# PV matmuls of two steps in one block, bf16 pieces of the row maxima on GpSimd, and another order in the gating stage

## The reference, cut to what matters

```python
q, k, v = split(x @ W_qkv + b_qkv)            # 16 heads of 16
q, k = rope(q), rope(k)
att = where(causal, q @ k.T / 4, -1e9)
y = softmax(att) @ v @ W_proj + b_proj
x1 = layernorm(x + y)
probs = softmax(x1 @ gate_w.T); expert = argmax(probs)     # top 1 of 8
rank = cumsum(one_hot(expert)) - 1; keep = rank < 640
ffn = probs[expert] * (relu(x1[kept] @ w1 + b1) @ w2 + b2) # 0 for dropped tokens
out = layernorm(x1 + ffn)
```

## Time and profile before

| | us |
|---|---|
| median of 3 runs (lowest, highest) | 1422.44 (1416.7, 1422.6) |
| the profiled execution | 1421.05 |
| its span, first to last instruction | 1419.3 |
| mean granted TensorE clock | 0.94 |
| TensorE busy | 1271.5 (90%) |
| VectorE busy | 1158.4 (82%) |
| ScalarE busy | 777.7 (55%) |
| GpSimd busy | 230.3 (16%) |

### The profile page before, as it was taken

How to read it: one execution, slowest core, us unless ns; L and a number is a source line. 1 busy time by engine, 2 the same in 40 slices (tenths; PEclk the granted TensorE clock), 3 DMA queues, 4 the chain that set the end, 5 groups by cost and what they waited for, 6 DMA issues and landing times. The chain is left out here.

```text
span 1419.3 us, 22655 instructions
## 1 busy us (share of the span) xinstructions
PE 1271.5 (90%) x7857; PEld 644.2 (45%) x7857; DVE 1158.4 (82%) x2780; ACT 777.7 (55%) x1098; POOL 230.3 (16%) x250
## 2 busy tenths in 40 slices
PE   8892997999999999999999999999578739999997
PEld 4550132333333333333333333332366539999997
DVE  6994997999999999899899999991276728888886
ACT  2441065666666666666666667668245435544442
POOL 1336000100100100101101100101234321111221
PEclk9995599999999999999999999999888859999999
DMA  6877496131131131121221210000545422343330
GB/s 206 255 240 167 62 155 146 31 90 32 31 91 31 33 88 32 48 74 31 61 60 32 75 46 10 23 2 16 165 142 181 154 92 93 101 142 117 96 105 21
DMA packets 120272, 126.91 MB, mean 89 GB/s; under 512 B 16604, under 2 KB 102751, under 8 KB 120160
## 3 DMA queue, kind: packets, MB, share of 16 engines
q1 hardware_dynamic: 116576, 117.01, 29.7%
q0 software_dynamic: 3584, 8.47, 1.7%
HBM read 83.02 MB, written 48.38 MB: 93 GB/s over the span
## 5 line engine op out<-in xcount | busy, mean ns | idle before, releaser
L625 ACT ACTIVATE probs<-scores 128x1024 f32<-128x1024 f32 (+3 forms) x640 | 539.0, 894 | 327.9 <-PE scores L518 327.0
L680 DVE TENSOR_REDUCE part_max<-ring 128x1 f32<-128x512 f32 x768 | 478.4, 684 | 24.0 <-PE ring L548 22.4
L548 PE MATMUL ring<-k_stack,q_stack 96*128 96x512 bf16 (+3 forms) x1280 | 407.1, 363 | 41.1 <-DMA k_stack<-pieces_d 26.2
L518 PE MATMUL scores<-q_stack,k_stack 99*128 99x512 bf16 (+3 forms) x1280 | 339.8, 350 | 9.9 <-DMA q_stack<-max_rows 7.6
L534 PE MATMUL out_p<-probs,v_s 128*32 128x512 f32 (+3 forms) x2560 | 300.2, 541 | 0.5 <-POOL probs L730 0.3
L548 PEld LDWEIGHTS ring<-k_stack,q_stack 96*128 96x128 bf16 x1280 | 114.9, 97 | 347.9 <-DVE part_max L680 148.7
L674 DVE CUSTOM_DVE_ANT_0 scratch<-ring,mask_s 128x384 f32<-128x384 f32 (+2 forms) x384 | 195.0, 551 | 18.0 <-issue 17.1
L730 POOL TENSOR_SCALAR_AFFINE_SELECT probs<-probs 128x512 f32<-128x512 f32 x128 | 81.6, 637 | 781.8 <-ACT probs L625 781.8
L518 PEld LDWEIGHTS scores<-q_stack,k_stack 99*128 99x128 bf16 x1280 | 113.0, 98 | 182.7 <-issue 64.3
L1394 PE MATMUL psY<-w_hi,h_hi 128*128 128x256 f32 x320 | 90.9, 284 | 0.0
L534 PEld LDWEIGHTS out_p<-probs,v_s 128*32 128x32 f32 x2560 | 50.6, 108 | 87.3 <-issue 56.2
(11 more groups left out here) (113 smaller groups left out, 1349.9 us busy)
## 6 DMA issues: line engine op xcount, KB each, us to landing
w_whole<-w SPq DMA_DIRECT2D x16, 1024.0 KB, 7.5
q_stack<-pieces_d SPq DMA_DIRECT2D x192, 64.0 KB, 3.0
k_stack<-pieces_d SPq DMA_DIRECT2D x192, 64.0 KB, 3.1
v_d<-vt SPq DMA_DIRECT2D x8, 1024.0 KB, 4.6
v_s<-v_d SPq DMA_DIRECT2D x8, 1024.0 KB, 6.0
o_d<-o_s SPq DMA_DIRECT2D x32, 256.0 KB, 2.2
p_o<-o_d SPq DMA_DIRECT2D x8, 1024.0 KB, 6.0
slots_d<-no_row SPq DMA_DIRECT2D x1, 5200.0 KB, 28.3
```

Source lines behind the costliest of these rows:

```text
L518: last = nc.tensor.matmul(scores[p][:, hh, off:CHUNK], k_stack[i][0:KROWS, kb // TPC, j, kb % TPC * P:(kb % TPC + 1) * P], q_stack[i][0:KR ...
L548: last = nc.tensor.matmul(slot[:, h * w:(h + 1) * w], q_stack[i][0:SROWS, qt // TPC, j + h, qt % TPC * P:(qt % TPC + 1) * P], k_stack[i][0 ...
L625: nc.scalar.activation(probs[n % NPROB][:, 2 * p:2 * p + 2, off:CHUNK], scores[p][:, :, off:CHUNK], ACT.Exp, scale=SCALE).then_inc(exp_don ...
L680: nc.vector.tensor_reduce(part_max[:, qt, j, t:t + 1], ring[m % 3][:, 0:w], axis=AX.X, op=ALU.max).then_inc(ring_read, 1)
```

## The change

1. *PV.* `step` no longer calls PV for the step two before in every step. In each odd step it calls `pv_pair`, which runs PV for two steps one behind the other; even steps have none. `copy_o` on ScalarE moves from behind a step's two exponentials to between the two of the next step.
2. *Pieces.* VectorE only negates the turned maxima into SBUF (`negate_maxima`) and gives the ring slot back. GpSimd makes the three pieces (`cut_maxima`), placed in its stream by `PLAN`, behind the mask of the same step. SP waits for GpSimd's last piece instead of for the ring.
3. *Gating stage.* On ScalarE `deviations` is split; the second root stands behind the next chunk's first `copy_yT`, and `copy_x1T` and the plain rows are arranged anew. On VectorE `norm_chunk` goes ahead of `place`, and the next chunk's first `normalise` ahead of `choose`. On TensorE the next chunk's first `turn_o` goes ahead of the logits.

TensorE's order in the first unit, from one PV block on, before: two rows with `out_p` are the PV blocks of single steps (four heads each); `ring` are ring items, `scores` the scores of a step.

The diff:

```diff
@@ -326,7 +326,8 @@
 LAG = 2
-assert NSTEP % NPROB == 0
+PAIR = 2
+assert NSTEP % NPROB == 0 and all(last % PAIR == PAIR - 1 for last in LAST)
@@ -399,6 +400,7 @@
         row_max = [sb(f"row_max{c}", [P, NMAXROW]) for c in range(NCH)]
+        max_neg = [sb(f"max_neg{c}", [NMAXROW, P]) for c in range(NCH)]
         max_rest = sb("max_rest", [NMAXROW, P])
@@ -425,7 +427,7 @@
         MAX_PRIMED = [1 + MAX_DMAS] + [1] * (NCH - 1)
-        N_CUT = NPIECE
+        N_CUT = NPIECE + 1
@@ -449,9 +451,9 @@
-            def load_max(c, i, read):
...
-                sp.wait_ge(ring_read, read)
+            def load_max(c, i, uses):
...
+                sp.wait_ge(max_cut[c], N_CUT * uses)
                 for pc in range(NPIECE):
@@ -464,16 +466,16 @@
                 for c in (2, 1):
-                    load_max(c, i, NRING * u + TURN_AT[c] + 1)
+                    load_max(c, i, u + 1)
                 store_o(u, b, g, 3)
...
                     load_chunk(two_ahead[0], two_ahead[1], i, 3)
-                load_max(0, i, NRING * (u + 1) + (1 if last else TURN_AT[0] + 1))
+                load_max(0, i, u + 2)
                 store_o(u, b, g, 2)
...
                 if not last:
-                    load_max(3, 1 - i, NRING * (u + 1) + TURN_AT[3] + 1)
+                    load_max(3, 1 - i, u + 2)
                 for c in (1, 0):
@@ -486,7 +488,7 @@
             load_v(0, 0, 0)
-            load_max(3, 0, TURN_AT[3] + 1)
+            load_max(3, 0, 1)
             for c in ORDER:
@@ -587,20 +589,25 @@
                 if behind:
-                    pv_step(*behind)
+                    pv_pair(*behind)
                 items(u, i, uses, third, stop, ahead)
...
+            def pv_pair(u, i, n):
...
+                for m in range(n - PAIR + 1, n + 1):
+                    pv_step(u, i, m)
...
                         pe.wait_ge(v_loaded[i], 16 * uses[0])
-                    step(u, i, uses, n, ahead, (u, i, n - LAG))
-                for n in range(NSTEP - LAG, NSTEP):
-                    if ahead:
-                        step(u + 1, 1 - i, uses[1:], n + LAG - NSTEP, ahead, (u, i, n))
-                    else:
-                        pv_step(u, i, n)
+                    step(u, i, uses, n, ahead, (u, i, n - LAG) if n % PAIR else None)
+                if ahead:
+                    for n in range(LAG):
+                        step(u + 1, 1 - i, uses[1:], n, ahead, (u, i, NSTEP + n - LAG) if n % PAIR else None)
+                else:
+                    pv_pair(u, i, NSTEP - 1)
@@ -618,6 +625,12 @@
                 for p in range(2):
+                    if p == 1:
+                        if n == LAG and u:
+                            copy_o(u - 1, 0)
+                        for c in ORDER:
+                            if n - LAG - 1 == LAST[c]:
+                                copy_o(u, c)
                     act.wait_ge(scores_ready[p], NSTEP * u + n + 1)
@@ -630,18 +643,9 @@
-            def unit(u, follows):
+            for u in range(UNITS):
                 for n in range(NSTEP):
                     exp_step(u, n)
-                    if n == LAG - 1 and follows:
-                        copy_o(u - 1, 0)
-                    for c in ORDER:
-                        if n - LAG == LAST[c]:
-                            copy_o(u, c)
...
-            unit(0, False)
-            for u in range(1, UNITS):
-                unit(u, True)
             copy_o(UNITS - 1, 0)
@@ -688,47 +692,61 @@
-            def cut_maxima(c, u, m):
-                turned = ring[m % 3][0:NMAXROW, 0:P]
-                first, second, third = (rows[:] for rows in max_rows[c])
+            def negate_maxima(c, u, m):
+                if u:
+                    dve.wait_ge(max_cut[c], N_CUT * u)
                 dve.wait_ge(ring_full, NRING * u + m + 1)
...
-                dve.wait_ge(max_loaded[c], 1 + MAX_DMAS * u)
-                nc.vector.tensor_scalar(first, turned, -1.0, None, ALU.mult).then_inc(max_cut[c], 1)
-                dve.wait_ge(max_cut[c], N_CUT * u + 1)
-                nc.vector.scalar_tensor_tensor(max_rest[:], turned, -1.0, first,
-                                               ALU.mult, ALU.subtract).then_inc(max_cut[c], 1)
-                dve.wait_ge(max_cut[c], N_CUT * u + 2)
-                nc.vector.tensor_copy(second, max_rest[:]).then_inc(max_cut[c], 1)
-                dve.wait_ge(max_cut[c], N_CUT * u + 3)
-                nc.vector.tensor_tensor(third, max_rest[:], second, ALU.subtract).then_inc(ring_read, 1)
+                nc.vector.tensor_scalar(max_neg[c][:], ring[m % 3][0:NMAXROW, 0:P], -1.0, None,
+                                        ALU.mult).then_inc(ring_read, 1)
...
                     if isinstance(item, int):
-                        cut_maxima(item, u, m)
+                        negate_maxima(item, u, m)
                     else:
...
                         fold(u, FOLD_AFTER[m], m)
-            cut_maxima(0, UNITS, 0)
+            negate_maxima(0, UNITS, 0)
...
                 nc.gpsimd.memset(k_stack[i][SROWS:KROWS], 1.0).then_inc(ones_set, 1)
+            pool.wait_ge(const_loaded, 16 * 2)
...
+            def cut_maxima(c, u, m):
+                first, second, third = (rows[:] for rows in max_rows[c])
+                pool.wait_ge(max_loaded[c], 1 + MAX_DMAS * u)
+                pool.wait_ge(ring_read, NRING * u + m + 1)
+                nc.gpsimd.tensor_copy(first, max_neg[c][:]).then_inc(max_cut[c], 1)
+                pool.wait_ge(max_cut[c], N_CUT * u + 1)
+                nc.gpsimd.tensor_tensor(max_rest[:], max_neg[c][:], first, ALU.subtract).then_inc(max_cut[c], 1)
+                pool.wait_ge(max_cut[c], N_CUT * u + 2)
+                nc.gpsimd.tensor_copy(second, max_rest[:]).then_inc(max_cut[c], 1)
+                pool.wait_ge(max_cut[c], N_CUT * u + 3)
+                nc.gpsimd.tensor_tensor(third, max_rest[:], second, ALU.subtract).then_inc(max_cut[c], 1)
...
+            def mask(u, n):
+                off = STEPS[n][2]
+                for p in range(2):
+                    pool.wait_ge(exp_done[p], NSTEP * u + n + 1)
+                block_ = probs[n % NPROB][:, :, off:off + P]
+                nc.gpsimd.affine_select(out=block_, in_=block_, compare_op=ALU.is_ge, fill=0.0, base=0,
+                                        pattern=[[0, HPU], [1, P]], channel_multiplier=-1).then_inc(masked, 1)
...
+            for m in range(LEAD):
+                if isinstance(ITEMS[m], int):
+                    cut_maxima(ITEMS[m], 0, m)
             for u in range(0, UNITS):
-                for d, n in enumerate(DIAG):
-                    off = STEPS[n][2]
-                    done = in_register(pool, NSTEP * u + n + 1)
-                    pool.wait_ge(const_loaded, 16 * 2)
-                    for p in range(2):
-                        pool.wait_ge(exp_done[p], done)
...
-                    block_ = probs[n % NPROB][:, :, off:off + P]
-                    nc.gpsimd.affine_select(out=block_, in_=block_, compare_op=ALU.is_ge, fill=0.0, base=0,
-                                            pattern=[[0, HPU], [1, P]], channel_multiplier=-1).then_inc(masked, 1)
+                for n, (first, stop) in enumerate(PLAN):
+                    if n in DIAG:
+                        mask(u, n)
+                    for m in range(first, stop):
+                        v, k = u + m // NRING, m % NRING
+                        if isinstance(ITEMS[k], int) and (v < UNITS or k == TURN_AT[0]):
+                            cut_maxima(ITEMS[k], v, k if v < UNITS else 0)
@@ -973,10 +991,11 @@
                 project(n, 2)
+                if h_next is not None:
+                    turn_o(n + 1, 1 - i, h_next, 0)
                 gate_logits(n - 1)
...
                 if h_next is not None:
-                    turn_o(n + 1, 1 - i, h_next, 0)
                     turn_o(n + 1, 1 - i, h_next, 1)
@@ -1007,9 +1026,11 @@
-            def deviations(n, i):
+            def first_root(n, i):
                 act.wait_ge(mv_ready, TPC * (n + 1))
                 nc.scalar.activation(std[i][:], mv[i][:, :, 1], ACT.Sqrt, bias=eps_s[:]).then_inc(std_ready, 1)
...
+            def second_root(n, i):
                 act.wait_ge(var_step, 2 * (n + 1))
@@ -1033,22 +1054,24 @@
                 copy_yT(n, 0)
+                second_root(n - 1, 1 - i)
+                copy_yT(n, 1)
                 plain_rows(n - 1, 1 - i, h_before, (0, 1))
-                copy_yT(n, 1)
+                copy_yT(n, 2)
                 plain_rows(n - 1, 1 - i, h_before, (2, 3))
-                copy_yT(n, 2)
                 copy_x1T(n - 1)
...
                 exponentials(n - 1)
-                deviations(n, i)
+                first_root(n, i)
...
                 copy_yT(0, t)
-            deviations(0, 0)
+            first_root(0, 0)
             for k in range(0, NC3 // 2 - 1):
...
             both(NC3 - 1, 1, NC3 // 2 - 1)
+            second_root(NC3 - 1, 1)
             copy_x1T(NC3 - 1)
```

(7 more changed lines are left out.)

## The result

The changed kernel takes 1462.12 us (median of 4, 1461.33 to 1463.82) against 1422.41: a ratio of 1.0281, 95% interval 1.026 to 1.0302. It is slower, and by the forecast's amount (1461). Its span is 1460.9 us at a mean granted clock of 0.945.

The account below looks back on a forecast made before the run. TensorE and VectorE were taken to bound each other through three ring slots. From 1421.1 us, +46.2 (units 0 to 6), -2.6, +3.3, +5.0, -1.7 and -12.0 (gating) gave 1459.3, median 1461, range 1434 to 1486.

Parts of the forecast that it names:

- What bounds: Attention: TensorE and VectorE hold each other through three ring slots; a backlog of 1.34 us just covers a 1.00 block.
- Hand-over against backlog: Steady attention units: double blocks of 1.86 us leave VectorE dry 0.94 each, 14.2 a unit; unit 109.4, +6.6.
- Hand-overs gained: Attention PV: 160 fewer blocks save TensorE 0.19 us each, 3.8 a unit, 30 in all.
- Unit 0: First attention unit: scores already wait 7.56 us for a DMA of the maxima, which hides lateness, -2.6 us.
- Unit 7: Last attention unit: +3.3 us from ring work, +5.0 from exponentials, two steps taking 5.0 instead of 4.18.
- Pieces: Maxima's pieces on GpSimd: VectorE saves 3.4 us a unit; a cut takes GpSimd 1.2 (0.4 to 2.6) and fits.
- Gating: Gating stage: shorter waits give 1.7 us a chunk, -12 for seven; chunks of 13.4, VectorE late next.
- The total: Whole kernel: the terms sum to 1459.3 us for the profiled execution; the median is 1.4 above, 1461.
- TensorE as the bound: Attention: TensorE catches up after each block, so saved hand-overs and other cuts give 1365 to 1385 us; chance 0.08.
- second rival: Attention: VectorE's dry times fall in idle already there, +0.4 to +3 us a unit, about 1423 (1415 to 1438); chance 0.12.
- third rival: Slower than the sum: late cuts, all idle stays, +10.8 us a unit, about 1496; TensorE perhaps granted less clock; chance 0.10.

Follow-up runs that it names:

- e12: The kernel before, single PV blocks, with two ring slots instead of three: 1543.14 us, ratio 1.0843.
- e6: The kernel before with plain reductions reading 128 of 512 columns, so maxima leave out the rest: 1390.16 us, one run.
- e7: The changed kernel with plain reductions reading 128 of 512 columns: 1402.86 us, one run.
- e1: The changed kernel with PV in one block a step again and output copies in their old place: 1407.54 us, ratio 0.9899.
- e2: The kernel before with double PV blocks and the moved copies alone, old pieces and gating stage: 1489.21 us, ratio 1.0469.

## Why the prediction was right

- *What bounds.* Two engines in lockstep through three slots: supported by e12, which changed only the slots.
- *Hand-over against backlog.* The block is 1.85 long (1.86 predicted), the gap 0.87 (0.94). VectorE's idle in a unit was put at 14.2 + 2.1 + 1.3 = 17.6 and is 18.3; its busy time at 91.8 and is 90.9. The sum, 109.4, met 108.9 to 109.3. Its make-up is another, though. Behind the twelve blocks of two full steps the trace has 11.4 us in sum for the 11.3 predicted, but from 0.30 to 1.24 each; behind the four of 512 and 384 columns it has 4.9 (0.71 to 1.92 each) for 2.9. That is 16.2 for 14.2, while the 3.4 us of issue and paired reductions that were held as now have shrunk: all other idle time of the unit is 2.0. Most of the one error cancels against the other and against the 0.9 of busy time; this much of the fit is luck.
- *Hand-overs gained.* They weren't in the sum, rightly. A double block does take 1.85 us for 2 x 1.00, but no unit got shorter by the 3.8 us, not even with VectorE's reductions short: TensorE's busy time in a unit fell by 1.0 (100.01 in e6, 99.00 in e7).
- *Unit 0.* 1.3 us of the wait for the DMA were hidden (7.56 to 6.26), not 2.6; the rest of the miss, +6.3 for +4.0, stays open.
- *Unit 7.* 4.92 for the 5.0 of two steps; +9.3 for +8.3.
- *Pieces.* GpSimd needs 0.42, 0.28, 0.42 and 0.28, 1.4 us a cut for the 1.2 taken. It fitted: only one of the seven later units began with a wait for the pieces, of 0.16 us. Without the double blocks it doesn't fit: the cover was the slowness itself. VectorE's busy time fell by 4.3 us a unit for 3.4, with single blocks (e1) by 3.1.
- *Gating.* -11.0 for -12; chunks of 13.7 for 13.4, and VectorE late next, as named.
- *The total.* The profiled executions are 41.7 us apart (1421.05 and 1462.72) where the sum had 38.2: six steady units came out 2.4 us under it, unit 0, unit 7, the start and the gating stage together 5.0 over. That the medians meet at 1461 and 1462 owes another 2 us to which executions were profiled.
- *Rivals.* TensorE as the bound falls with e2. Of the second rival a part is true: VectorE's idle time grew by 10.6 us a unit for gaps of 16.2, so a third of them fell in idle time that was there anyway; two thirds didn't. The third rival's clock stayed at 1.00 with TensorE busy for 102.18 of 109.15 us.

## What to carry to other kernels

Before joining work of one kind into longer blocks on the producing engine, compare the block, with all else that feeds the consumer nothing, to what the buffer still holds of the consumer's work at the moment the block starts (here 1.34 us), less the time from the start of the first item behind the block to the consumer's start on it (here 0.42). If the block is longer, expect each one to cost about the difference, whatever the producer saves. And test each part of a joint change alone: here one part hid the 13 us that the other two are worth together (e1), and a late transfer too.

## What the runs showed beyond that

GpSimd's subtraction of 128 columns takes 0.42 us where one of 512 takes 1.16; by length alone it would be 0.29. A straight line through the two gives, as an estimate, 0.17 us that don't depend on length, if the number of partitions (16 and 128) doesn't matter. A wait of TensorE can be followed by a lower clock: in e1, behind the 2.19 us on the DMA, two score matmuls took 1.06 us for the usual 0.60, and the granted clock of the next 3 us (599 to 602) was 0.56, most of it at the lower of the two levels. TensorE was busy for 102.05 us in that unit, against 100.57 to 100.73 in e1's other five.
